# One attention layer with a routed feed-forward: the period of the main loop written in another order

## What is computed

```python
k = x @ W_lat + b_lat
q = (x @ W_d + b_d).reshape(Bx, Tx, NH, L)          # NH = 16 heads, L = 128
att = jnp.einsum('bhtl,bsl->bhts', q, k) * scale
att = jnp.where(causal[None, None], att, -jnp.inf)
att = jax.nn.softmax(att, axis=-1)
y = jnp.einsum('bhts,bsl->bhtl', att, k)
return y @ W_proj + b_proj                          # summed over the heads
```

## Time and profile before

| | us |
|---|---|
| median of 3 runs | 280.72 (280.70 to 280.82) |
| profiled execution, whole | 280.79 |
| span of its trace | 279.1 |
| PE busy | 271.6 (97%) |
| DVE busy | 218.8 (78%) |
| ACT busy | 212.1 (76%) |
| POOL busy | 153.9 (55%) |

### The profile page before, as it was taken

One profiled execution on the slowest core, in us unless ns is written; L12 is line 12 of the kernel. 1 busy time (PEld: TensorE's weight loads), 2 busy tenths in 40 slices (PEclk: granted clock), 3 DMA queues, 4 the chain that ended last, 5 costly groups with the idle time before them and its releaser, 6 DMA issues.

```text
span 279.1 us, 6206 instructions
## 1 busy us (share of the span) xinstructions
PE 271.6 (97%) x1885; PEld 247.2 (89%) x1885; DVE 218.8 (78%) x701; ACT 212.1 (76%) x578; POOL 153.9 (55%) x214
## 2 busy tenths in 40 slices
PE   8999999999999999999999999999999999999991
PEld 4878999999999998999999999999999999999990
DVE  2698777777777777788789888899988887779882
ACT  3689877777787778887787877787777778879471
POOL 6468444444443336555666866665657847238652
PEclk9999999999999999999999999999999999999997
DMA  6593111011101111111111111110112200020151
GB/s 184 137 305 112 39 40 34 27 33 38 34 24 36 38 39 38 40 38 42 38 38 40 38 41 38 39 37 22 38 38 79 78 21 21 1 77 1 58 171 38
DMA packets 18842, 15.53 MB, mean 56 GB/s; under 512 B 1641, under 2 KB 18178, under 8 KB 18818
## 3 DMA queue, kind: packets, MB, share of 16 engines
q1 hardware_dynamic: 18242, 13.65, 16.8%
q0 software_dynamic: 576, 1.58, 1.6%
HBM read 12.60 MB, written 2.63 MB: 55 GB/s over the span
## 4 chain that ended last, share of the span: by engine, by line
PE 97%; DVE 0%; POOLq 0%; issue 0%; ACT 0%; DVEq 0%
PE bank L412 21%; PE bank L414 20%; PE bank L413 20%; PE bank L547 9%; PE ps_out L412 7%; PE ps_out L413 6%; PE ps_out L414 6%; PE bank L527 3%; PE bank L637 3%; PE bank L470 1%; PE bank L424 1%; POOLq L60 0%; PE bank L676 0%; PE bank L678 0%; PE bank L557 0%
## 5 line engine op out<-in xcount | busy, mean ns | idle before, releaser
L841 ACT ACTIVATE probs<-probs,negmax 128x512 f32<-128x512 f32 (+3 forms) x128 | 72.6, 576 | 5.7 <-DVE negmax L1026 4.3
L1384 POOL TENSOR_TENSOR wd_hi<-wd_raw,zero 128x256 fp32r<-128x256 f32 x31 | 23.7, 766 | 87.9 <-DVE probs L1098 84.7
L849 ACT CAST pT_hi<-bank 128x512 fp32r<-128x512 f32 (+2 forms) x96 | 43.4, 488 | 28.1 <-PE bank L547 27.7
L1026 DVE CUSTOM_DVE_ANT_0 probs<-bank,mask_row 128x512 f32<-128x512 f32 (+3 forms) x128 | 59.2, 482 | 0.7 <-PE bank L504 0.7
L1035 DVE TENSOR_TENSOR pT_lo<-bank,pT_hi 128x512 fp32r<-128x512 f32 (+2 forms) x96 | 52.8, 552 | 6.1 <-ACT pT_hi L849 5.5
L547 PEld LDWEIGHTS bank<-ident_r,prob_words 128*128 128x128 f32 x310 | 33.0, 140 | 5.5 <-ACT probs L893 0.4
L412 PE MATMUL ps_out<-wp_hi,yT_hi 128*128 128x256 f32 x124 | 37.1, 299 | 0.0
L412 PE MATMUL bank<-kT_hi,qT_hi 128*128 128x256 f32 (+2 forms) x94 | 36.5, 388 | 0.0
L413 PE MATMUL ps_out<-wp_lo,yT_hi 128*128 128x256 f32 x124 | 35.0, 282 | 0.0
L414 PE MATMUL ps_out<-wp_hi,yT_lo 128*128 128x256 f32 x124 | 35.0, 282 | 0.0
L1055 DVE TENSOR_TENSOR yT_lo<-bank,yT_hi 128x512 fp32r<-128x512 f32 x31 | 21.4, 690 | 15.8 <-PE bank L414 13.6
(11 more groups left out here) (203 smaller groups left out, 731.8 us busy)
## 6 DMA issues: line engine op xcount, KB each, us to landing
wd_raw<-in_L_attn_W_d SPq DMA_DIRECT2D x32, 128.0 KB, 2.2
wp_raw<-in_L_attn_W_proj SPq DMA_DIRECT2D x32, 128.0 KB, 2.1
wf_raw<-in_L_ffn_w SPq DMA_DIRECT2D x2, 1024.0 KB, 6.4
x_nat<-in_L_attn_x SPq DMA_DIRECT2D x4, 256.0 KB, 2.9
out<-z_all SPq DMA_DIRECT2D x4, 256.0 KB, 2.3
picked<-ranked SPq DMA_DIRECT2D x2, 258.0 KB, 2.8
wlat_raw<-in_L_attn_W_lat SPq DMA_DIRECT2D x1, 128.0 KB, 3.5
bproj_all<-in_L_attn_b_proj SPq DMA_DIRECT2D x1, 128.0 KB, 3.6
```

What stands on the lines that cost most here:

```text
L841: act.activation(p_tile(s, j), p_tile(s, j), ACT.Exp, bias=negmax[:, s, j:j + 1], scale=-1.0, accum_out=sums[:, s, j:j + 1]).then_inc(exp_ ...
L849: act.copy(pT_hi[:, dst], src).then_inc(pt_hi_done, 1)
L1026: dve.tensor_tensor_reduce(p_tile(s, j), score_bank[j], mask_row[:, (TILES - 1 - j) * P:], -SCALE, -MASKED, ALU.add, ALU.min, accum_out=ne ...
L1384: pool.tensor_tensor(hi, src, nothing, ALU.add).then_inc(hi_done, 1)
```

## The change

For 28 periods, `ONE_RUN` (2 to 30 without 18), each of PE, ACT and DVE gets a written order of its own (`one_run`). The other periods keep `period`; the list `LATE` goes. On PE: scores 3, 2, 1, 0, the ten turnings in one run, projection, queries, values. Turning 2 goes into `ps_s3`, behind DVE's maximum of tile 3, and the queries go into `ps_s10`, behind all four maxima. In the period after such a one tile 3's third product alone waits for the queries' low part, and tile 1 waits until the queries have been taken out of its bank. On ACT the exponential of tile 3 stands ahead of the copies of the turnings, and the split of the queries stands behind all exponentials. On DVE yT's low part is cut in two halves around the maximum of tile 3, and both pieces of side work stand at the end.

```diff
+        def query_bank(period):
+            return ps_y if period <= 0 else ps_s10 if period in ONE_RUN else ps_s3
...
-        LATE = (2, AT_STATS_2, AT_COMPARE_2, AT_REST_2)
+        ONE_RUN = tuple(q for q in range(2, UNITS - 1) if q != AT_STATS)
...
+                if n == 2 and at.fixed in ONE_RUN:
+                    dst = ps_s3
+                    wait(pe, negmax_done, p * 4 + 1)
+                else:
+                    wait(pe, pt_lo_done, p * 3 - (3, 4, 2)[n])
...
-                    wait(pe, negmax_done, at.p * 4 + 1)
-                dst = ps_q_first if at.fixed == 0 else ps_q
+                    wait(pe, negmax_done, at.p * 4 + (4 if at.fixed in ONE_RUN else 1))
+                dst = query_bank(at.fixed)
...
+            def one_run(at):
+                scores(at, (3, 2))
+                scores(at, (1, 0))
+                for n in range(3):
+                    turn(at, n)
+                if at.fixed == AT_K:
+                    turn_k(1)
+                if at.fixed == AT_PICKED:
+                    turn_picked()
+                project(at)
+                queries(at)
+                values(at)
...
+            def one_run(at):
+                if at.fixed == 2:
+                    kT_bias(1)
+                y_high(at)
+                if at.fixed - 1 == AT_TURN:
+                    row_of_scores(0, ps_t1)
+                exps(at, (3,))
+                for n in range(3):
+                    turned(at, n)
...
+                exps(at, (2, 1, 0))
+                split_queries(at.p + 1, at.place(1), at.head(1), at.fixed)
+                normalize(at)
...
+            def one_run(at):
+                p = at.p
+                if at.fixed - 1 == AT_RANK:
+                    ranks(0, ps_t1)
+                wait(dve, scores_ready, p * 3 + 1)
+                wait(dve, y_hi_done, p - 1)
+                y_low(slice(0, KEEP))
+                maxima(at, (3,))
+                wait(dve, scores_ready, p * 3 + 2)
+                y_low(slice(KEEP, SEQ)).then_inc(y_lo_done, 1)
+                maxima(at, (2,))
+                wait(dve, scores_ready, p * 3 + 3)
+                turned(at, 0)
+                maxima(at, (1, 0))
+                turned(at, 1)
+                turned(at, 2)
...
+                normalize(at)
+                queries_low(p + 1, at.place(1), at.head(1), at.fixed)
+                middle_piece(at)
+                last_piece(at)
```

More of the change, by code:

```diff
@@ L482, in _ @@
             for c in range(CH):
-                last = product(ps_q_first[:, :], (wd_hi[0][:, c, :], wd_lo[0][:, c, :]),
+                last = product(ps_y[:, :], (wd_hi[0][:, c, :], wd_lo[0][:, c, :]),
                                (xT_hi[0][:, c, :], xT_lo[0][:, c, :]), c == 0, c == CH - 1)
@@ L514, in scores @@
                         pe.wait_ge(kT_done, 2)
+                apart = at.fixed - 1 in ONE_RUN
                 for j in js:
@@ L517, in scores @@
                     dst = score_bank[j]
+                    t = slice(j * P, (j + 1) * P)
                     if j == 3:
-                        wait(pe, q_lo_done, p + 1)
+                        wait(pe, q_hi_done if apart else q_lo_done, p + 1)
                     if j:
                         wait(pe, negmax_done, p * 4 - {3: 3, 2: 2, 1: 0}[j])
-                    t = slice(j * P, (j + 1) * P)
-                    if j:
+                    if j == 1 and apart:
+                        wait(pe, q_first_done, p + 1)
+                    if j == 3 and apart:
+                        pe.matmul(dst, qT_hi[s][:, t], kT_hi[b][:, 0:n], start=True, stop=False)
+                        pe.matmul(dst, qT_hi[s][:, t], kT_lo[b][:, 0:n], start=False, stop=False)
+                        wait(pe, q_lo_done, p + 1)
+                        last = pe.matmul(dst, qT_lo[s][:, t], kT_hi[b][:, 0:n], start=False, stop=True)
+                    elif j:
                         last = product(dst, (qT_hi[s][:, t], qT_lo[s][:, t]), (kT_hi[b][:, 0:n], kT_lo[b][:, 0:n]))
@@ L979, in queries_low @@
             def queries_low(k, place, head, period):
-                src = ps_q_first if period <= 0 else ps_q
+                src = query_bank(period)
                 wait(dve, q_hi_done, k + 1)
@@ L1038, in turned, with normalize, y_low @@
                     dve.tensor_copy(pT_last[:, :], ps_s3[:, 0:P]).then_inc(pt_last_done, 1)
-            def period(at):
+            def normalize(at):
+                s = at.place(0)
+                wait(dve, exp_done, at.p * 4 + 4)
+                dve.reciprocal(rinv[:, s, :], sums[:, s, :]).then_inc(rinv_done, 1)
+                wait(dve, rinv_done, at.p + 1)
+                for j in (2, 1, 0):
+                    dve.tensor_scalar(p_tile(s, j), p_tile(s, j), rinv[:, s, j:j + 1], None,
+                                      ALU.mult).then_inc(norm_dve, 1)
+            def y_low(part):
+                return dve.tensor_tensor(yT_lo[:, part], ps_y[:, part], yT_hi[:, part].bitcast(F32), ALU.subtract)
+            def one_run(at):
                 p = at.p
@@ L1056, in period @@
                                       ALU.subtract).then_inc(y_lo_done, 1)
-                if at.live(0) and at.fixed not in LATE:
+                if at.live(0):
                     maxima(at, (3,))
@@ L1090, in period @@
                     turned(at, 2)
-                s = at.place(0)
                 if at.live(0):
[L1093 to L1097, removed]
-                        dve.tensor_scalar(p_tile(s, j), p_tile(s, j), rinv[:, s, j:j + 1], None,
-                                          ALU.mult).then_inc(norm_dve, 1)
+                    normalize(at)
                 last_piece(at)
```

92 lines of the change are left out of this document (47 added, 45 removed).

## The result

| kernel, on the same chip | median | range of 6 runs | profiled span |
|---|---|---|---|
| before | 280.77 us | 280.61 to 280.9 us | 279.1 us |
| after | 304.03 us | 303.87 to 304.2 us | 302.3 us |

The changed kernel takes 1.0824 times the time of the kernel before (95% interval 1.0814 to 1.0835): 23.3 us more. The forecast was 297.0 us, with a range from 290.5 to 304.0. The direction and the mechanism were right. The size was 7 us short: the median lies 0.03 us above the upper end of the range, less than its own runs differ, so it stands at the very edge.

A forecast was written before the change was run, and what follows sets the result against it. PE bounds the kernel before; the new order makes its queries wait on DVE and ACT. 15.7 (waits, less junctions) + 1.3 (side work) - 0.7 (extra turnings) = 16.3 us more, giving 297.0 us, range 290.5 to 304.

The forecast's parts named there:

- What bounds: Before the change PE bounds, busy 7.00 of 7.00 us in the loop; DVE and ACT decide nothing.
- the junctions: On PE, joining four runs of short instructions into two saves 0.03 us a period, 0.8 us over 28 periods.
- the full tails: On PE, upper bound for joining short runs: 0.16 us a period, 4.5 us over 28 periods.
- The chain: DVE and ACT work up to all four row maxima makes PE's queries wait 0.59 us; period 0.56 longer, 15.7 in all.
- the last handover: From DVE's maxima of tiles 1 and 0 to PE's queries: 0.05 us.
- The lower bound of the wait: Smallest wait of PE at the queries, from bounds on handovers and the half low part: 0.43 us.
- The side work: DVE's layer norm and router pieces, moved to the period's end, delay the next chain after periods 24 and 25: +1.3 us.
- The room of 1.1 us at the period's end: On DVE, between the end of qT_lo and the next chain, about 1.1 us of pieces fit for nothing.
- The extra turnings: Four extra turnings each in periods 14 (k) and 30 (picked rows) fall into PE's waiting time: -0.7 us.
- PE as the bound: Rival: with a chain 0.6 us shorter, queries find their bank free; 279.9 us, 276.2 with full tails; chance 0.05.
- The query loop: Rival: the queries' split reaches the next scores late, past a 0.45 us margin; 307 us if 0.8 late; chance 0.06.
- The clock: Rival: PE's clock falls with its pauses and ten turnings; half clock in one period in ten gives 317 us; chance 0.02.

The follow-up runs named there:

- Maxima first: Changed kernel with DVE's maxima of tiles 1 and 0 ahead of turning 0's low part: 284.76 us, 1.0151 times the kernel before.
- turning 0 first: Changed kernel with ACT's copy of turning 0 ahead of the exponential of tile 3: 291.67 us, 1.0388 times the kernel before.
- Splits later: Changed kernel with GpSimd's splits behind periods 24 and 25 held back until DVE's comparisons are over: 301.71 us, 1.074 times the kernel before.

## Why the prediction was right, and where its size was off

*What bounds, and the junctions.* Right. The forecast of 0.03 us a period for joining short runs came out at 0.018 in the loop and at nothing in period 13, and the 0.16 of the full tails was not there. (The tail that is called 0.07 in one place is the 0.08 of the sentences before it.) The ten turnings take 0.089 each with their tail.

*The chain.* Right to 0.04 us in every link up to the last maximum, and its consequences as listed: PE's load idle 28 times, 17.4 us (17 forecast); PE at 92%; ACT's high part straight behind the exponential; DVE idle 0.62 ahead of its low part; the wait feeding itself. Maxima first and turning 0 first show it as a cause. The term was a little small: 0.60 us in the loop instead of 0.56, and 0.69 in the 17 written-out periods behind it, where PE's query product carries two waits and the last handover took 0.15 instead of 0.05. That is 28 x 0.60 + 17 x 0.09 = 18.3 instead of 15.7. The lower bound of the wait, 0.43, does not follow from the terms given for it (0.59 - 0.06 - 0.04 is 0.49); nothing came to hang on it, since the wait was longer than forecast.

*The side work: the step that failed.* It stood at +1.3 us, for periods 24 and 25. Beyond what the common period grew by, the trace has 1.5 in period 25, 0.9 in 26, 0.6 and 0.45 in 22 and 23, 1.0 in 16 and 1.1 in 2, some 5.6 us. Three things were missing.
- The durations in the earlier trace rows belong to the old place. The 0.75 and 0.61 were taken where GpSimd was all but idle or began later than the piece, and the pieces were moved to where GpSimd runs. The rows to be seen for this were in the trace of before. The third row of that group, 0.70 for 128x4 elements, is four times its 0.17 alone. And GpSimd's split that began during the second took 1.04 there instead of 0.73:

```profile
191.31 1.04 POOL L1384 TENSOR_TENSOR wd_hi<-wd_raw,zero 128x256 fp32r<-128x256 f32 x1 [2.95 <-DVE probs L1098]
192.43 0.73 POOL L1386 TENSOR_TENSOR wd_lo<-wd_raw,wd_hi 128x256 fp32r<-128x256 f32 x1
```

  The prediction looked at whom GpSimd's splits release, not at what they run beside. Splits later puts this at 2.3 us for two periods. The room of 1.1 us at the period's end was right: with 1.28 us of pieces, period 25 is 0.2 over the common one.
- Periods 21 and 22 have pieces too (router products, 0.77 to 0.95 each in their new place), which I left out.
- The same move took the low part of k behind PE's next scores (period 16), and ACT's copy of k ahead of the chain (period 2). I walked the queues for the common period and not for the periods with extra work.

*The extra turnings.* Forecast -0.7; periods 14 and 30 came out 0.5 and 0.3 under the common growth, -0.9.

The sum is then 18.3 + 5.6 - 0.9 = 23.0, and the periods of the trace grow by 23.1. That the total still fell on the edge of the range was in part luck: the side work and the extra turnings together came to 4.7, outside their own bounds of 0 to 3, and the chain used only 2.6 of the 4.5 us that it was allowed.

*The rivals.* PE as the bound did not come, but by one exchange on DVE it does, which is the 0.6 us of chain that this rival asked for. The query loop kept its margin: no score product waits on qT_lo in the loop. The clock stayed at full speed with ten turnings in a run and a pause of 0.5 us in each period; it is the 1.00 in the row of period 13 (busy us of PE, PEld, DVE, ACT, POOL; clock, DMA, GB/s):

```profile
109.97:118.00 8.03, 7.57 (x54) 6.87 (x52) 5.80 (x19) 5.81 (x18) 5.11 (x13) 1.00 0.12 34
```

The Trainium skill ("TensorE: Matmul & The Clock Gate", part 4) says that the full clock does not engage for transposes. No slice here shows that, but the ten turnings are 0.89 us of a period of 8.03, so no run here shows what transposes alone would do.

## What to carry to other kernels

When a buffer is passed on earlier, follow the new wait back through every engine's written order: the instruction that frees the buffer may stand behind something that hangs on a third engine, and one exchange there can be worth most of the loss (here two maxima ahead of DVE's low part of a turning, 19.3 of 23.3 us). Then walk the exceptional periods as carefully as the common one, since a move applies to the pieces that stand only there. And price a moved instruction by a row taken beside the same neighbours, not by its row in the old place.

## What the runs showed of the hardware

- VectorE's small SBUF instructions beside GpSimd's splits: 128x4 elements in 0.69 us instead of 0.17, 128x128 in 0.82 instead of 0.35, 128x512 in 1.04 instead of 0.74; GpSimd's 128x256 split 1.18 instead of 0.73. In these rows the one that begins later ends a fixed time behind the other's end (0.55 for 128x512, 0.42 for 128x384, 0.02 for 128x4, 0.6 for a split), so the small ones lose the most, in proportion.
- A second semaphore wait at the TensorE instruction that ends a pause cost 0.06 us in a written-out period (13: 8.026 to 7.962), and put the wait under "issue" in the profile.
- Ten transposes in one run behind an fp32 pair take 0.089 us each at a granted clock of 1.00, with the tail in them (0.89 us in period 13).
